# A 512-column bias product for the second layer of an edge network, in place of four 128-column ones

## What is computed

```python
edge_input = jnp.concatenate([x[row], x[col], edge_attr, d_raw], axis=-1)
h = jax.nn.silu(edge_input @ ew1 + eb1)
m_ij = jax.nn.silu(h @ ew2 + eb2)
agg = jax.ops.segment_sum(m_ij, row, num_segments=x.shape[0])
```

## Time and profile before

| | us |
|---|---|
| median of 3 runs | 10843.75 (10837.68 to 10864.26) |
| profiled execution, whole | 10854.43 |
| its span, first to last instruction | 10852.7 |
| PE busy | 6041.0 (56%) |
| PEld busy | 5018.0 (46%) |
| VectorE busy | 5269.9 (49%) |
| ScalarE busy | 2228.0 (21%) |
| GpSimd busy | 3588.3 (33%) |

### The profile page before, as it was taken

The page is one execution under the profiler, slowest core; times in us unless marked ns, Lnnn a source line. Parts: engine busy times, 40 slices in busy tenths (PEclk is TensorE's granted clock), DMA queues, the critical chain, the costliest instruction groups (busy, mean ns, idle before and its releaser), DMA issues. The chain is left out here.

```text
span 10852.7 us, 167129 instructions
## 1 busy us (share of the span) xinstructions
PE 6041.0 (56%) x43186; PEld 5018.0 (46%) x43187; DVE 5269.9 (49%) x9074; ACT 2228.0 (21%) x4530; POOL 3588.3 (33%) x3345
## 2 busy tenths in 40 slices
PE   0122333333331566665137767677888888788696
PEld 0122333333331311111037667577777777777496
DVE  6666333333331699999224454333333333333344
ACT  0465000000000244444420000111221111121132
POOL 0000777777777000000000000245555554555000
PEclk9999999999999856566568788798999998999697
DMA  0200222222222222222145557222222222222263
GB/s 21 101 0 8 41 40 40 40 40 40 40 40 26 41 52 52 52 52 52 52 165 220 227 219 273 64 75 77 78 77 78 78 78 75 77 79 79 40 222 118
DMA packets 1450866, 876.35 MB, mean 81 GB/s; under 512 B 905023, under 2 KB 1376596, under 8 KB 1425535
## 3 DMA queue, kind: packets, MB, share of 16 engines
q1 hardware_dynamic: 1237570, 639.77, 20.6%
q0 software_dynamic: 106048, 137.48, 6.0%
q10 hardware_dynamic: 107136, 97.57, 2.6%
HBM read 713.06 MB, written 159.27 MB: 80 GB/s over the span
## 5 line engine op out<-in xcount | busy, mean ns | idle before, releaser
L653 POOL DMA_INDIRECT out_records<-scatter_recs,scatter_rows x1650 | 1964.3, 1190 | 1194.4 <-issue 1193.8
L1567 POOL DMA_INDIRECT edge_mlp_b_rows<-b_table,edge_mlp_recs x1664 | 1613.7, 970 | 2045.3 <-DMA edge_mlp_recs<-out_records 1512.9
L712 PE MATMUL scatter_sum<-scatter_attr,scatter_hot 128*128 128x65 f32 x3328 | 810.3, 422 | 1508.0 <-DMA scatter_attr<-in_edge_attr 1244.0
L712 PEld LDWEIGHTS scatter_sum<-scatter_attr,scatter_hot 128*128 128x128 f32 x3328 | 741.0, 328 | 1577.4 <-DMA scatter_attr<-in_edge_attr 1164.5
L1027 PE MATMUL pairs_p_ring<-pairs_hot_near,pairs_hot_far 128*128 128x512 f16 x2256 | 958.2, 575 | 726.3 <-ACT pairs_p_ring L1046 630.3
L1010 DVE TENSOR_TENSOR pairs_hot_near<-c_iota_wide,pairs_shift 128x4096 f16<-128x4096 f16 x282 | 1245.3, 4416 | 0.0
L1682 DVE CAST edge_mlp_hot_t<-edge_mlp_p_hot 128x512 f32<-128x512 bf16 x416 | 287.8, 692 | 1746.5 <-DMA edge_counts<-pairs_cells 979.7
L1027 PEld LDWEIGHTS pairs_p_ring<-pairs_hot_near,pairs_hot_far 128*128 128x128 bf16 x2256 | 276.0, 122 | 1407.7 <-issue 1372.1
L1621 PE MATMUL edge_mlp_p_pre<-edge_mlp_hot_t,edge_mlp_a_blk 128*128 128x128 f32 x3328 | 755.0, 313 | 299.9 <-DVE edge_mlp_hot_t L1682 143.0
L760 DVE TENSOR_TENSOR nodes_wide_sums<-nodes_wide_sums,scatter_sum 128x65 f32 x1664 | 386.0, 232 | 1011.1 <-issue 868.5
L1104 POOL MEMSET sum_x_parts<- 128x192 bf16 x2 | 0.5, 260 | 2444.3 <-POOLq L123 2444.3
(11 more groups left out here) (419 smaller groups left out, 9269.9 us busy)
## 6 DMA issues: line engine op xcount, KB each, us to landing
sum_x_tiles<-edge_counts SPq DMA_DIRECT2D x78, 1536.0 KB, 7.4
edge_mlp_a_blk<-a_table SPq DMA_DIRECT2D x1664, 64.0 KB
edge_counts<-pairs_cells ACTq DMA_DIRECT2D x744, 128.0 KB, 1.7
sum_z_tiles<-edge_counts SPq DMA_DIRECT2D x48, 1920.0 KB, 7.8
sum_y_tiles<-edge_counts SPq DMA_DIRECT2D x39, 1536.0 KB, 7.6
scatter_attr<-in_edge_attr SPq DMA_DIRECT2D x1664, 32.0 KB
sum_x_tiles<-edge_counts SPq DMA_DIRECT2D x26, 1664.0 KB, 9.8
pairs_ends<-out_records SPq DMA_DIRECT2D x2256, 1.0 KB, 1.6
```

Of the source, the lines that this page charges most:

```text
L653: pool.indirect_dma_start(out=out_rec, out_offset=bass.IndirectOffsetOnAxis(ap=rows[s][:, c:c + 1], axis=0), in_=recs[s][:, c], in_offset= ...
L712: mm = pe.matmul(psum[s][:, c, 0:F + 1], hot[s][:, c], attr[s][:, c], start=True, stop=True)
L1567: pool.indirect_dma_start(out=b_rows[s][:, c], out_offset=None, in_=b_tab, in_offset=bass.IndirectOffsetOnAxis(ap=recs[s][:, c, FE + 1:FE ...
```

## The change

Before the loop VectorE copies `b2_split` four times side by side into a new tile `b2_group`, of 512 columns. In `second` one bf16 product of `ones_b` by `b2_group` comes first and writes the whole bank of `p_m` (`start=True`), and the four products by `w2_sb` add to it (`start=False`). The wait for `h` stays ahead of both. `skip_group_check=True` is an option of the program that builds the kernel and no instruction.

```diff
@@ edge_mlp
         b2_part, b2_split, ones_b = sb("b2_part", [P, H], BF16), sb("b2_split", [P, H], BF16), sb("ones_b", [P, P], BF16)
+        b2_group = sb("b2_group", [P, G, H], BF16)
...
-        SPLITS = 4 + 3 * 3
+        SPLITS = 4 + 3 * 3 + 1
...
                 pe.wait_ge(h_made, it * SLOTS + s + 1)
+                pe.matmul(p_m[:], ones_b[:], b2_group[:], start=True, stop=False, skip_group_check=True)
                 for c in range(G):
-                    pe.matmul(p_m[:, c], h[:, c], w2_sb[:], start=True, stop=False)
-                    mm = pe.matmul(p_m[:, c], ones_b[:], b2_split[:], start=False, stop=True)
+                    mm = pe.matmul(p_m[:, c], h[:, c], w2_sb[:], start=False, stop=True, skip_group_check=True)
                 mm.then_inc(m_pre, 1)
...
                 step(dve.tensor_tensor(b2_rows[:], b2_rows[:], b2_part[:], ALU.subtract))
+            step(dve.tensor_copy(b2_group[:], bc(b2_split[:], 1, G)))
             assert step.n == SPLITS
```

## The result

The change made the kernel slower: 10913.4 us (median of 6 runs, 10904.2 to 10941.6) against 10840.9 us (6 runs, 10828.7 to 10868.0), a ratio of 1.0066 with a 95% interval of 1.0047 to 1.0084. A gain of 45 us was forecast. Later, on another chip, the same two kernels stood at 0.991: there the change gains 86 us.

The account below looks back on a forecast made before the run. TensorE's chain of work with its hand-overs bounds the edge network stage; 211 groups saving 0.27 us each give 57 us, less a fifth, so 45 us off 10843.75, about 10799 us; 8 in 10 between 10741 and 10871.

Parts of the forecast that it names:

- What bounds the kernel: Edge network stage, 3166 us: bound by TensorE's chain of work with hand-overs to ScalarE and VectorE, not by loads.
- 2.37 us in a group: Edge network stage: waiting and half clock, the difference between 7.61 us per group and 5.24 without a wait.
- a fifth of the 57 us: Part of the saving let be lost to hand-overs held up while GpSimd's gathers run, leaving a gain of 45 us.
- What a bias product costs: Second layer: each bias product takes a place of 0.111 us, four cost 0.444 us in a group at the higher clock.
- what the 512-column product costs: Second layer: one wide bias product takes 0.21 us at the higher clock, saving 0.23 us in a group.
- The price at the lower clock: Second layer at 1.2 GHz: four bias products 0.85 us, the wide one 0.42, saving 0.43 us in a group.
- Added work: One VectorE copy ahead of the loop, 512 bf16 elements in each partition, at most 0.69 us, once.
- What of the saving reaches the end: First layer: 205 of 416 groups wait and gain nothing; the other 211 keep 0.27 us each, 57 us, cut to 45.
- The holds absorb it: Rival: quick groups are followed by holds ending by the gathers' clock; under 33 us either way, 10811 to 10876; chance 0.33.
- Slower, by the clock: Rival: longer TensorE waits bring the lower clock more often; at 0.88 slower by some 35 us, 10880; chance 0.14.
- the 0.89 that the prediction had named as a sign: TensorE's clock column in the stage, 0.91 before: a fall below 0.89 would show that the clock did it.
- the 27 that I had set: Edge network stage: each 0.01 less of TensorE's clock costs 27 us, on 2180 us of full-clock work.

Follow-up runs that it names:

- e8_change_again: The changed kernel, no edit, on a chip where hand-overs are not held up: 9783.4 us against 9868.9 for the kernel before, 0.9910.
- e2: The changed kernel with GpSimd's gathers made only for the first four groups: 9779.0 us, 0.8979 of the kernel before.
- e4: The changed kernel with the wide bias product issued twice, same result: 10884.8 us, 0.9997 of the kernel before.
- f3: The kernel before with only the four products by the gathered rows moved ahead of the wait for hot_t: 10881.8 us, 1.0038 of the kernel before.
- e3: The changed kernel with four bias products of 128 columns in a row in place of the wide one: 10931.7 us, 1.0032 of the kernel before.
- f's chip: A chip with holds, kernel before 10849.9 us; the unedited change ran there again: 10894.6 us, 1.0052.
- f2: The changed kernel with the bias ahead of the wait for h and the gathered-row products ahead of the wait for hot_t: 10841.0 us, 0.9996 of the kernel before.

## Why the prediction failed

**What bounds the kernel.** Right in so far as TensorE does not wait for loaded data, and GpSimd still waits for records; but the gathers cost 970 to 1010 us in another way, by the holds. Half right on TensorE: the profile showed the holds as TensorE's waits and, in part, as its lower clock. The prediction saw them, 2.37 us in a group, and named the gathers as a possible cause, but took off only "a fifth of the 57 us" for them.

**What a bias product costs, what the 512-column product costs.** Right at the higher clock. A place is 0.111 us, the wide product takes 0.22, not 0.21, and a group went from 5.24 to 5.02 us. The gain of 97 us without gathers and 86 on a chip without holds fits 416 x 0.23 = 96. The price at the lower clock was not tested by itself; the second layer as a whole gave 130 us where 112 were forecast. This also decides between the rows and the Trainium skill (TensorE: Matmul & The Clock Gate, section Back-to-back issue gap): its 131 ns for a product of 512 columns in a stream of load and product pairs is not what these runs show. Its formula for a matmul by itself, N / 2.4 + 2.5 ns, gives 216 ns, and that is the median distance from the wide product to the next one in the trace of the changed kernel and in that of `e8_change_again`. There it stands alone between products of another kind; but the long stream of the earlier trace rows, 15 products of 192 columns 82 ns apart, each with its load, is met by that formula too.

**Added work.** The copy takes 0.29 us, once. Right.

**What of the saving reaches the end.** This step failed. It sorted the groups of one trace into those that wait ahead of the first layer and those that don't, and let the second kind keep their saving: "the remaining 211 groups give 211 x 0.27 = 57 us", less "a fifth of the 57 us". It took the holds as given: of their length it said that it "does not hang on the length of the second layer". In the new trace the waits ahead of the first layer are as many but 162 us longer, where some 40 more were forecast, and that is more than the 130 us by which the second layer is shorter in all groups together. The step treated a wait as a property of a group, when it is the outcome of two streams, TensorE's hand-overs and GpSimd's gathers, each of which starts the other. Replaying the old waits with one of the streams shifted did not give the new ones.

**The rivals.** "The holds absorb it" had the mechanism and the wrong end: I let it take all, not more than all. "Slower, by the clock" had the right sign. The clock did fall, to 0.88, below the 0.89 that the prediction had named as a sign. Over 413 groups the time at 1.2 GHz rose from 561 to 769 us, but only 115 of the 208 us more lie in TensorE's products (480 to 595) and the rest in waits; at half the speed 115 us cost about 57, which is 19 us for each 0.01 and not the 27 that I had set. It did not make the loss alone. At full clock the groups have 92 us less work, 413 x 0.222, and the time above that work grew by 151 us (993 to 1144): by this estimate 57 through the clock and some 95 through longer waits. Either of them alone would have left the change level or ahead. That the clock fell because the waits grew is argued: e2, with the same shortened work and no holds, has a granted clock of 1.00. The Trainium skill (the same page, section HAM oscillation) has it that a stream broken by waits falls back to its lower clock; the step from 0.91 to 0.88 beside 162 us more of waiting agrees.

**What is shown and what is open.** Shown: the change takes 0.22 us off each group and is a gain of 0.9% where hand-overs are not held up; on three of six occasions, the first included, they were held up, and on the two where the gathers were taken from GpSimd the holds and some 1000 us went with them; with holds the change costs 0.5 to 0.7%, seen in its trace as longer waits ahead of the first layer and a lower clock; a second layer shortened by other instructions loses too, and one filled up to its old length does not. Open is why the holds grow by more than is saved. Crowding (theory Q) is my best reading: in the changed kernel a quick group takes 5.02 us and its four gathers 5.0, so those of two groups run into one another, and long and quick groups alternate more sharply. The traces agree. Of 1664 gathers 173 stood in unbroken runs of more than four before, and 435 do with the change (starts at most 1.4 us apart; with 1.7 as the limit it is 435 and 591). The hand-overs of the transposes that fell into such long runs went from 30, late by 61 us together, to 64, late by 248; those in the other runs went from 625 us to 527. So all of the growth, 89 us in this hand-over, is in the long runs. The same count is 283 in e4, which is level, 374 in f3 and 413 in e3, which lose 0.3 to 0.4%, and 459 in the change on f's chip; f2, level with 668, does not fit. But that is one trace of each kernel, and long runs may follow from long holds as well as cause them; the runs with half of the gathers never met such a chip, so the cause stays open. And f3, slower by 0.4% at the old amount of work, says that on such a chip the order of the work matters as well as its amount. Also open is what sets the occasions with holds apart from those without.

## What to carry to other kernels

When a trace shows an engine idle with its input long made, find out what holds it before pricing anything behind it: remove the suspect (here one loop of gathers) and see if a thousand microseconds go. A saving on an engine that alternates with such holds was not carried by a replay of the old waits here, and even its sign came out wrong, so it belongs to a wide range or to an experiment. And a short bf16 product between float32 ones cost as much as the float32 weight load behind it, 0.111 us, and not its own 0.056, so gathering four of them into one wide one was worth half of their price here (0.444 to 0.22 us), where nothing else was in the way.

## What was not expected of the hardware

- The same kernel takes 9861 to 9879 us on three of the occasions and 10828 to 10927 on the others, with nothing between, and within an occasion it is always one of the two.
- On the slower occasions TensorE's semaphore updates reach VectorE up to 7.5 us late and ScalarE up to 5.9 while GpSimd makes indirect DMAs; with the same bytes moved by SyncE both start 0.04 us behind TensorE. On the faster occasions a running gather does no such harm.
- In the changed kernel's trace 208 of the 416 wide products have no record on PE, while all 416 of their weight loads are there; so such a product is priced by the start of the next one.
